# A two-layer graph network kernel: four edge buffers and whole-block vector work, a batched three-step search, nodes laid out 128 by 98, and ScalarE copying one bank of transposed rows

## The reference

```python
h = jnp.maximum(_layernorm(x, axis=-1), 0.0)
# layer 0: a gated MLP over every edge's features, summed by destination
h1 = silu(edge_attr @ W1 + b1);  v = silu(h1 @ W2 + b2)
g1 = silu(edge_attr @ G1 + g1_); g = sigmoid(g1 @ G2 + g2)
x = x + h + segment_sum(v * g, dst, 12500)
# layer 1: attention over the edges
h = jnp.maximum(_layernorm(x, axis=-1), 0.0)
s, r = h @ Ws + bs, h @ Wr + br
logits = einsum(mish(s[src] + r[dst]), aw) + ab     # 4 heads of 16
alpha = segment_softmax(logits, dst)
x = x + h + segment_sum(alpha * s[src], dst)
```

## Time and profile before

| | us |
|---|---|
| median of 3 runs | 6303.33 (6302.56 to 6303.81) |
| the profiled execution, its own time | 6302.94 |
| the profiled execution, span of its trace | 6301.1 |
| edge_mlp up to the barrier | 0 to 1702.5 |
| of it: blocks with search, blocks without | 29 to 955, 955 to 1690 |
| update_nodes up to the barrier | 1702.5 to 2036.3 |
| attention | 2036.3 to 6129.4 |
| finish | 6129.4 to 6301.1 |
| busy over the span: DVE, POOL, ACT, PE | 4619.8, 3544.2, 2838.6, 1251.4 |

### The profile page before, as it was taken

How to read it: one execution, slowest core, us unless ns; L and a number is a source line. 1 busy time by engine, 2 the same in 40 slices (tenths; PEclk the granted TensorE clock), 3 DMA queues, 4 the chain that set the end, 5 groups by cost and what they waited for, 6 DMA issues and landing times. The chain is left out here.

```text
span 6301.1 us, 45975 instructions
## 1 busy us (share of the span) xinstructions
PE 1251.4 (20%) x8389; PEld 527.7 (8%) x8389; DVE 4619.8 (73%) x4935; ACT 2838.6 (45%) x3154; POOL 3544.2 (56%) x3660
## 2 busy tenths in 40 slices
PE   5666677777521000000000000000000000000000
PEld 2222222322221000000000000000000000000000
DVE  6777776666653687778778877887778777878771
ACT  4555555666400444444444444444444444444430
POOL 1111110000087777777777777777777777777757
PEclk8889888888855555555555555555555555555555
DMA  5556555555422223322332232223322332232211
GB/s 170 185 182 186 181 184 173 169 167 172 145 53 57 68 79 83 86 79 79 87 82 79 79 90 80 79 79 83 86 79 79 88 82 79 79 90 79 79 56 44
DMA packets 317016, 655.20 MB, mean 104 GB/s; under 512 B 114338, under 2 KB 114340, under 8 KB 316747
## 3 DMA queue, kind: packets, MB, share of 16 engines
q1 hardware_dynamic: 188153, 508.07, 25.2%
q0 software_dynamic: 126720, 146.75, 11.1%
q10 hardware_dynamic: 2128, 0.23, 0.0%
HBM read 415.07 MB, written 239.34 MB: 104 GB/s over the span
## 5 line engine op out<-in xcount | busy, mean ns | idle before, releaser
L873 POOL DMA_INDIRECT se<-s_proj,idx x3168 | 2992.5, 945 | 965.4 <-issue 959.6
L891 ACT ACTIVATE held_ps<-r_keep 128x1536 f32 (+1 forms) x135 | 196.3, 1454 | 1463.3 <-DVE z L974 1423.7
L1112 PE MATMUL a_ps<-r_ident,r_state 128*4 128x128 f32 x1 | 0.4, 375 | 4125.9 <-DVE drop L1141 4125.9
L974 DVE TENSOR_TENSOR z<-se,held_ps 128x1536 f32<-128x1536 f32 x135 | 369.9, 2740 | 454.6 <-DMA se<-s_proj,idx 417.5
L308 ACT ACTIVATE hidden<-h_ps,r_b1g 128x1024 f32<-128x1024 f32 x404 | 450.3, 1115 | 468.9 <-PE h_ps L258 468.0
L258 PE MATMUL h_ps<-edges,r_w1g 64*64 64x512 f32 x3232 | 540.7, 737 | 417.3 <-DMA edges<-in_edge_attr 401.4
L362 DVE SCALAR_TENSOR_TENSOR msg<-gate,value 128x512 f32<-128x512 f32 x404 | 277.0, 686 | 450.0 <-ACT gate L317 436.8
L489 POOL DMA_INDIRECT block_of<-in_dst,block_id x106 | 105.7, 997 | 844.8 <-DVE block_id L396 844.8
L938 ACT ACTIVATE arows<-work_ps 128x1632 f32<-128x1632 f32 x135 | 206.8, 1532 | 740.8 <-DVEq L1010 740.8
L999 DVE TENSOR_TENSOR wse<-se,ex_ps 128x1536 f32<-128x1536 f32 x135 | 373.6, 2767 | 201.3 <-ACT ex_ps L929 201.3
L378 DVE TENSOR_TENSOR_SCAN sums<-keepb,sums,msg 128x512 f32<-128x512 bf16 x403 | 515.7, 1280 | 7.1
(11 more groups left out here) (180 smaller groups left out, 4313.0 us busy)
## 6 DMA issues: line engine op xcount, KB each, us to landing
states<-arows SPq DMA_DIRECT2D x135, 864.0 KB, 6.9
rs<-sums SPq DMA_DIRECT2D x135, 768.0 KB, 5.2
edges<-in_edge_attr SPq DMA_DIRECT2D x202, 512.0 KB, 4.3
sums<-rows SPq DMA_DIRECT2D x402, 256.0 KB, 2.6
keepb<-keep SPq DMA_DIRECT2D x404, 128.0 KB, 2.9
se<-s_proj,idx POOLq DMA_INDIRECT x3168
x_tile<-in_x SPq DMA_DIRECT2D x10, 312.5 KB
s_proj<-sr SPq DMA_DIRECT2D x10, 312.5 KB
```

Source lines behind the costliest of these rows:

```text
L873: pool.indirect_dma_start(out=se[b][:, k, :], out_offset=None, in_=D["s_proj"], in_offset=bass.IndirectOffsetOnAxis(ap=node[:, k:k + 1], a ...
L974: nc.vector.tensor_tensor(z[b][:, :, :], se[b][:, :, :].rearrange("p k f -> p f k"), rneg, ALU.subtract).then_inc(z_ready, 1)
```

## The change

Edges, masks and sums get four buffers each, and SyncE loads edges four blocks ahead and masks three. `product` and `scan` handle a whole block of 1,024 columns in one instruction each. `turn_rows` now transposes the block before the last one. Of the two banks of transposed rows VectorE copies one, right after the product, and ScalarE the other, for block c-3 between `outs` and `hid` of block c.

The search has three steps instead of two, and handles six columns of nodes at once (`Q`): 75 first samples, then one row of 55 samples per node, then one row of 100 destinations per node. `find_first`, `find_second` and `find_third` are each one comparison into `below` and one sum; each loop iteration of four blocks holds all three, for three different groups. GpSimd fetches with six gathers for the second step and six for the third. There are 17 groups (102 columns). The small operations after the search stand ahead of the last four blocks. The samples are loaded as 75 by 55 single values instead of 125 by 6.

Nodes lie on 128 partitions by 98 columns, in 14 steps of seven; x and the result are padded to 12,544 rows. The attention stage has no change in its code.

The diff, cut to its core; behind the sizes stand, in this order, the new step of SyncE, of TensorE, ScalarE's copy and step, VectorE's search (called after step j of four), and GpSimd's queue.

```diff
-NP, NJ = 125, 100
-JB = 10
+NP, NJ = P, 98
+JB = 7
-SB, SL, SP_ = 750, 550, 125
-NC = CH - 2
+S1, S2, S3 = 75, 55, 100
+Q = 6
+NC = 102
...
+            def step(c, m, first=False, last=False):
+                if not last:
+                    sp.wait_ge(h_ready, (c + 1) * 2)
+                    load(c + 4, m)
+                if not first:
+                    store(c - 2, m % 2)
+                if not last or c + 3 < NBLK:
+                    wait(sp, scanned, c)
+                    sp.sem_inc(sp_turn, 1)
+                    load_keep(c + 3, (m + 3) % 4)
...
+            def step(c, m, round, first=False, last=False):
+                for u in range(2):
+                    layer2(c, u)
+                    if not last:
+                        layer1(c + 1, (m + 1) % 4, u, round + (m + 1) // 4)
+                if not first:
+                    turn_rows(c - 2, (m + 2) % 4)
...
+            def to_rows(c, b, pair):
+                act.wait_ge(turned, c + 1)
+                wait(act, stored[b], pair * 32)
+                nc.scalar.activation(rows[b][:, :, J // 2:J, :].rearrange("p s j f -> p j s f"),
+                                     tr_ps[:, 1, :].rearrange("p (j s f) -> p j s f", s=2, f=F), ACT.Copy).then_inc(rows_ready, 1)
+            def step(c, m, pair, first=False, last=False):
+                hid(c, 1)
+                outs(c, m % 2, 0)
+                if not first:
+                    to_rows(c - 3, (m + 1) % 2, pair)
+                if not last:
+                    hid(c + 1, 0)
+                outs(c, m % 2, 1)
...
+            def search(i, j, first, second, third, n):
+                if third and j == 0:
+                    find_third(i - 2, n + 1)
+                if second and j == 1:
+                    find_second(i - 1, n + third + 1)
+                if first and j == 2:
+                    find_first(i, n + third + second + 1)
...
+            fetch(0, nodes2, D["samples"], block1, block1_known, nodes2_in)
+            with pool.Fori(1, NQ) as q:
+                fetch(q, nodes2, D["samples"], block1, block1_known, nodes2_in)
+                fetch(q - 1, nodes3, blocks3, block2, block2_known, nodes3_in)
+            fetch(NQ - 1, nodes3, blocks3, block2, block2_known, nodes3_in)
```

More of the change, by code:

```diff
@@ L221, in _ @@
             sp.dma_start(mid[:, :], row(dst[E2 - 1:E2 + 1]).to_broadcast([P, 2])).then_inc(dst_in, 16)
[L222 to L226, removed]
+            load(2, 2)
+            load(3, 3)
             sp.wait_ge(keep16_ready, 2)
@@ L232, in _ @@
             sp.wait_ge(zeros_ready, 1)
             sp.dma_start(D["sums"][E:P * RUN, :].rearrange("(p k) f -> p (k f)", p=PAD_P), zeros[0:PAD_P, 0:PAD]).then_inc(pads_out, 16)
[L234 to L237, removed]
+            for c in range(2):
+                step(c, c, first=True)
+            with sp.Fori(0, NI - 1) as i:
+                for j in range(4):
+                    step(i * 4 + (2 + j), (2 + j) % 4)
@@ L265, in layer2 @@
                 pe.sem_inc(pe_turn, 1)
-                hid = hidden[u % 2]
+                hid = hidden[u]
                 for s in range(2):
@@ L291, in _ @@
             pe.wait_ge(weights_in, 16 * WEIGHTS)
-            layer1(0, 0)
-            layer1(0, 1)
+            layer1(0, 0, 0, 0)
+            layer1(0, 0, 1, 0)
             pe.wait_ge(ident_steps, 2)
[L295 to L299, removed]
+            for c in range(2):
+                step(c, c, 0, first=True)
+            with pe.Fori(0, NI - 1) as i:
+                for j in range(4):
+                    step(i * 4 + (2 + j), (2 + j) % 4, i + j // 2)
@@ L316, in outs @@
                 act.wait_ge(g_ready, n + 1)
[L317 to L323, removed]
+                nc.scalar.activation(gate[b][:, half], g_ps[:, :], ACT.Tanh, scale=0.5, bias=g2[:, :]).then_inc(gated, 1)
+            def to_rows(c, b, pair):
[3 more added lines that the diff above has]
+                                     tr_ps[:, 1, :].rearrange("p (j s f) -> p j s f", s=2, f=F), ACT.Copy).then_inc(rows_ready, 1)
@@ new lines, in find_third, with body @@
+            def find_third(q, n):
+                dve.wait_ge(nodes3_in, q * (16 * Q) + 16 * Q)
+                count(nodes3[:, :, :], count3, q, S3, n)
+            def search(i, j, first, second, third, n):
[5 more added lines that the diff above has]
+                    find_first(i, n + third + second + 1)
+            def body(i, n, first=False, second=False, third=False):
+                early = isinstance(i, int) and i == 0
+                for j in range(4):
+                    step(i * 4 + (2 + j), (2 + j) % 4, i + j // 2, i * 2 + j // 2, second=early and j < 2)
+                    search(i, j, first, second, third, n)
@@ L418, in _, with step @@
+            def step(c, m, round, pair, first=False, second=False):
+                product(c, m % 2)
+                if not first:
+                    to_rows(c - 2, m % 2, pair, first=second)
+                scan(c, m, round, first=first and m == 0)
             nc.vector.memset(near[:, :], -1).then_inc(padded, 1)
```

309 lines of the change are left out of this document (156 added, 153 removed).

## The result

The changed kernel takes **5882.0 us** (median of 4 runs, 5881.6 to 5884.1), the kernel before beside it 6302.9: a ratio of 0.9335, 95% interval [0.9319, 0.9351]. The forecast was 5810, the range 5675 to 5945. The profiled execution took 5882.2 us, 5880.3 of it the span. The sum of the prediction was made on the trace of before, so I go through it stage by stage.

What follows compares the result with a forecast made beforehand. It took late edge loads and a lowered clock to bound the edge stage, and GpSimd's gathers update, attention and finish. From 6302.9 us, minus 410 (edge stage), 53 (update) and 30 (finish), it forecast 5810, range 5675 to 5945.

Steps and rivals of the forecast that it cites:

- Late loads gone, full clock, 5.56 us a block: Steady edge blocks: TensorE's wait for edges vanishes, clock is full, TensorE's chain sets 5.56 us per block, bounds 5.3 and 5.9.
- ScalarE's copy hidden: Edge blocks: ScalarE's copy costs nothing behind TensorE's transposes; without that cover 0.2 us per block, 30 us.
- The search's cycle: Edge stage's search: request, twelve gathers, steps and blocks close a 30.5 us turn per four blocks; 15 turns cost 124 us.
- the last wait: End of the search: one last wait after the 15 turns, about 5 us (0 to 9).
- held up by VectorE: Rival: VectorE delays the search's gathers, a cycle grows by 8 us at most, 120 in all, 5930 us; chance 0.10.
- The start: Start of the edge stage: first scan ends at 35.3 us, block 3's second `gate` at 40.5.
- its term of 4 for the start: Start of SyncE's queue: single-value samples and two more edge loads stand ahead, costing 4 us, bounds 0 and 12.
- 128 partitions: Update and finish: gathers of 128 rows run faster than those of 125, saving 53 us and 30 us.
- DMA engines as the bound: Rival, edge stage: if DMA gives only 182 GB/s, a block takes 7.14 us, 224 more, 6034 us; chance 0.08.
- Attention: 0: Attention stage: the same 3,240 gathers, so no change in time, 0 us.

Runs made afterwards that it cites:

- e3: Changed kernel with two edge buffers instead of four and loads two blocks ahead: 6771.8 us, ratio 0.9944 to the kernel before.
- e2: Changed kernel with both copies of the transposed rows on VectorE, ScalarE's copy removed: 6459.6 us, ratio 0.9501 to the kernel before.
- e10: e8 plus padding zeros stored from 60 partitions, and edges of blocks 4 and 5 issued before the samples wait: 6284.0 us, ratio 0.9231.
- e5: Changed kernel with each scan of 1,024 columns cut into two of 512: 5855.1 us, a single run.
- e4: Kernel before with only the node layout changed to 128 by 98, seven columns a step: 6219.0 us, ratio 0.9876.
- e8: Changed kernel with search groups of three instead of six and third-step gathers requested before second-step ones: 5689.5 us, ratio 0.9037.

## Why the prediction was right, and where it was off

The time lay in the range, 72 us over the forecast, and all of that is in the edge stage (+71.5): 15 at the start, 64 in the search, 8 back in the pace. By its own steps:

- **Late loads gone, full clock, 5.56 us a block: right.** 5.52 measured, -8 us in all. e3 shows that the buffers did it.
- **ScalarE's copy hidden: right**, at 0.60 us; by e2 it is even worth 11. In e10, once the search waits no longer, the kernel with it is 42 us slower than the one without, and why is open.
- **The search's cycle: right in mechanism, mis-sized.** Place, releaser and number of turns were as said. From block 3's product (55.8) to the last (1344.3) lie 195.5 us more than 198 blocks at 5.52 take, for 131.5 predicted: 15 turns at 12.1 over the pace and not 8.3 (57 us), and 14.6 instead of 7.5 for the last wait, the small operations and block 4. Of a turn 3.6 us are the twelve gathers' starts (17.74 for 14.1). I had taken 1.28 apiece from a kernel whose gathers met shorter scans (1.28 us) and came one at a time; here they meet a scan of 2.34. The row that warned was the maximum of 1.88, and it was put down as a rival at 0.10: "held up by VectorE". That rival's mechanism is shown (e5), its price is half of its bound. The forecast and this rival are thus both part of what happened.
- **The start: 15 us short.** Block 3's second `gate` ended at 55.7, not 40.5 (40.3 is the end of its first one). TensorE's order puts the first half of `layer1` of block 4 ahead of the second half of block 3, and block 4's edges were issued only at 38.6, behind SyncE's wait for the samples, so block 3's product came at 55.8. The prediction costed that queue only up to the first scan (30.5 measured, 33 predicted), and the 15 lie outside the bounds of 0 and 12 that it gave its term of 4 for the start. Its reading of the Trainium skill, page "DMA: Bandwidth & Descriptors", section "Rules for kernel authors", was that the sample load would hold the queue for 5.6 us. The page gives the descriptors, not the queue's time, and the load's own row does not bear the reading out: 1.10 for 4,125 single values, near the 1.02 of 750 before. But the load right behind it, the same in both kernels, took 4.03 for 1.20, with one more load of edges ahead as well; which of the two did that, and how long the samples took to land, no row here tells (two rows of the changed kernel, one of the kernel before):

```profile
1.67 1.10 SPq L222 DMA_DIRECT2D sample<-in_dst  x1
3.35 4.03 SPq L225 DMA_DIRECT2D dsti<-in_dst  x1
...
3.34 1.20 SPq L215 DMA_DIRECT2D dsti<-in_dst  x1
```

- **128 partitions: right**, -56 and -28 for -53 and -30 (e4). **DMA engines as the bound: wrong**, 248 GB/s in e8. **Attention: 0**, +2.5 measured.

So of the 420 us gained, some 325 hang on the edge buffers, 85 are the nodes'; and 188 more lay in the order and size of the batches of the search. What whole-block products and scans and the three-step search are worth by themselves, against the halves and the two steps of before, no run shows.

## What to carry to other kernels

When several batches of requests share one queue, write down the cycle that the queue closes: from a request through all that stands ahead of the answer it needs, and back through the work of the engine that asks. Issue first what is needed first, and size the batch so that a turn, with gathers at the length they have beside the vector work, fits into the compute that covers it; here two lines were worth 188 us. And cut or enlarge vector instructions with an eye on what they hold up: here fewer, longer ones with two inputs in SBUF lengthened the GpSimd gathers that started beside them.

## What the hardware showed that I had not expected

- A gather beside a VectorE scan of 1,024 columns mostly takes 2.49 us (3.02 in e2, where it starts with the scan), alone 0.94; it ends 0.75 us after the scan does. With scans of 512 in e5 none takes over 1.43; in the kernel before one took 1.88.
- The price of a gather falls with more rows: 125 rows 1.178 us, 128 rows 0.944.
- On one of two chips attention took some 500 us more for the same program, so totals of two chips can't be compared. There ScalarE also began 1.0 us late once in four blocks of e10, only while the search ran; the cause is open.
